# Three of eight output tiles: expert rows gated by diagonal matrices on TensorE, added in one VectorE instruction

## The reference

```python
xf = layernorm(x).reshape(-1, 512)                       # 1024 tokens
probs = softmax(gelu(xf @ wg1 + bg1) @ wg2 + bg2)[:, :20] # 20 experts
top_vals, top_idx = top_k(probs, 2)
gates = zeros((N, 20)).at[arange(N)[:, None], top_idx].set(top_vals)
for e in range(20):
    y = y + gates[:, e, None] * (xf @ We[e] + be[e])
x = x + y
```

## Time and profile before

| | |
|---|---|
| three timed runs | 677.53, 674.92, 677.24 us (median 677.24) |
| the profiled execution | 675.09 us |
| its span, first to last instruction | 673.2 us |
| TensorE busy | 642.6 us, 95% of the span |
| VectorE busy | 439.9 us, 65% |
| ScalarE busy | 327.2 us, 49% |
| GpSimd busy | 299.4 us, 44% |
| mean granted clock of TensorE | 0.985 of full speed |

### The profile page before, as it was taken

The page is one execution under the profiler, slowest core; times in us unless marked ns, Lnnn a source line. Parts: engine busy times, 40 slices in busy tenths (PEclk is TensorE's granted clock), DMA queues, the critical chain, the costliest instruction groups (busy, mean ns, idle before and its releaser), DMA issues.

```text
span 673.2 us, 16124 instructions
## 1 busy us (share of the span) xinstructions
PE 642.6 (95%) x6390; PEld 526.1 (78%) x6390; DVE 439.9 (65%) x999; ACT 327.2 (49%) x620; POOL 299.4 (44%) x265
## 2 busy tenths in 40 slices
PE   5999999999999999999999999999999999999980
PEld 5778888887888788887888788887778787788850
DVE  4865666666556555757555557454477678999976
ACT  4435453544434444444433426334355654899930
POOL 2215644366344644366344614612126157788520
PEclk9999999999999999999999999999999999999995
DMA  8512566545764456445753562220000497999729
GB/s 331 210 50 47 137 168 150 128 113 137 174 137 122 121 147 148 111 125 144 174 127 77 136 168 83 80 64 2 2 18 34 146 363 272 382 389 354 285 86 339
DMA packets 41817, 105.68 MB, mean 157 GB/s; under 512 B 8052, under 2 KB 8436, under 8 KB 40962
## 3 DMA queue, kind: packets, MB, share of 16 engines
q1 hardware_dynamic: 37330, 96.12, 48.5%
q0 software_dynamic: 4400, 8.41, 3.4%
HBM read 65.61 MB, written 11.34 MB: 114 GB/s over the span
## 4 chain that ended last, share of the span: by engine, by line
PE 91%; DVE 4%; DMA 2%; ACT 1%; issue 1%; POOL 0%; POOLq 0%; DVEq 0%; SPq 0%; ACTq 0%
PE bank L195 25%; PE bank L197 23%; PE bank L196 23%; PE bank L415 5%; PE bank L397 4%; PE bank L201 3%; DVE x_sb L1854 2%; PE bank L633 1%; PE bank L620 1%; PE bank L649 1%; DMA wr<-scratch_ys 1%; DMA raw<-in_wk 1%; DMA xi<-scratch_xn,row 1%; PE bank L447 1%; DVE stats L1580 0%
## 5 line engine op out<-in xcount | busy, mean ns | idle before, releaser
L1891 POOL TENSOR_SCALAR pp<-pp,rl 128x400 f32<-128x400 f32 x128 | 164.1, 1300 | 182.4 <-DVE rl L1359 182.4
L978 ACT ACTIVATE pp<-pp,acc 128x400 f32<-128x400 f32 x128 | 79.0, 619 | 66.6 <-DVE acc L1418 66.6
L1418 DVE CUSTOM_DVE_ANT_0 pp<-bank,cap 128x400 f32<-128x400 f32 x128 | 65.9, 571 | 50.9 <-PE bank L397 50.9
L195 PE MATMUL bank<-chi,wk 128*128 128x400 f32 x248 | 87.3, 352 | 0.0
L196 PE MATMUL bank<-clo,wk 128*128 128x400 f32 x248 | 85.5, 345 | 0.0
L197 PE MATMUL bank<-chi,wk 128*128 128x400 f32 x248 | 85.5, 345 | 0.0
L1410 DVE STREAM_TRANSPOSE raw<-pp 128x512 f32<-128x512 f32 x128 | 83.4, 688 | 2.2 <-POOL pp L1891 2.2
L195 PE MATMUL bank<-wv,chi 128*128 128x512 f32 x192 | 78.8, 410 | 0.0
L196 PE MATMUL bank<-wv,chi 128*128 128x512 f32 x192 | 75.4, 393 | 0.0
L197 PE MATMUL bank<-wv,clo 128*128 128x512 f32 x192 | 75.2, 392 | 0.0
L195 PE MATMUL bank<-wh,xu 128*128 128x512 f32 x144 | 59.7, 415 | 0.4 <-ACT hT L912 0.2
(11 more groups left out here) (268 smaller groups left out, 1333.6 us busy)
## 6 DMA issues: line engine op xcount, KB each, us to landing
pt<-raw SPq DMA_DIRECT2D x256, 128.0 KB, 2.4
wr<-in_We SPq DMA_DIRECT2D x13, 1024.0 KB, 12.1
craw<-in_ctx SPq DMA_DIRECT2D x15, 800.0 KB, 4.6
raw<-in_We SPq DMA_DIRECT2D x8, 1024.0 KB, 13.2
acc<-in_We SPq DMA_DIRECT2D x6, 1024.0 KB, 12.6
wr<-scratch_ys SPq DMA_DIRECT2D x8, 512.0 KB, 8.1
x_sb<-in_x SPq DMA_DIRECT2D x2, 1024.0 KB, 11.5
scratch_xn<-acc SPq DMA_DIRECT2D x8, 256.0 KB
```

Of the source, the lines that this page charges most:

```text
L195: pe.matmul(o, lhs[0], rhs[0], start=start, stop=False)
L978: act.activation(frame(p8), frame(p8), ACT.Exp, bias=bias, scale=-1.0, accum_out=total).then_inc(S["a_exp"], 1)
L1418: dve.tensor_tensor_reduce(out=frame(p8), in0=scores[:, p8 % 4, :], in1=cap[:, :], scale=-1.0, scalar=nm[:, b, p8:p8 + 1] if seg else 3e38 ...
L1891: pool.tensor_scalar(frame(p8), frame(p8), rl[:, n % 2, p8:p8 + 1], None, ALU.mult).then_inc(S["g_pn"], 1)
```

## The change

Three tiles of the eight, 2, 4 and 6 (`FULL`), are done in another way. ScalarE makes six 128x128 diagonal matrices after the last expert block: the identity scaled by the gates of row c of tile i. For a tile of `FULL`, TensorE puts the bias product into a bank of its own (3, 4 or 7) and leaves the sum open; when the gather of the tile has landed it adds two float32 products to it, diagonal times `yga[:, i, c]`. VectorE then adds the bank to `x_sb` in one instruction. The other five tiles (`plain`) are done as before. The order of the tiles on VectorE and of the output writes on SyncE becomes 0, 1, 3, 2, 5, 4, 7, 6; the order of the gathers stays 0 to 7. `spare` issues products that nobody reads: two behind each plain bias product, three ahead of each tile of `FULL`.

```diff
+        diag = [cs2[:, 128 * j:128 * j + 128] for j in range(4)] + [mbd[:, j, :] for j in range(2)]
+        FULL, ENDING = (2, 4, 6), (0, 1, 3, 2, 5, 4, 7, 6)
+        plain = [i for i in ENDING if i not in FULL]
...
-                def biases(which):
-                    for i in which:
-                        if i >= 3:
-                            pe.wait_ge(S["v_y"], i - 2)
-                        r = slice(32 * (i % 4), 32 * (i % 4) + E)
-                        pe.matmul(pb[i % 3][:, :], gT[r, i // 4, :], be[r, :], start=True, stop=True).then_inc(S["p_be"], 1)
+                def bias(i, bank, stop):
+                    r = slice(32 * (i % 4), 32 * (i % 4) + E)
+                    return pe.matmul(bank[:, :], gT[r, i // 4, :], be[r, :], start=True, stop=stop)
+
+                def spare(n, bank):
+
+                    for _ in range(n):
+                        pe.matmul(bank[:, :], wh[1][0][:, 0, 0:128], wh[1][0][:, 0, :], start=True, stop=True)
+
+                def ending():
+                    for n, i in enumerate(plain):
+                        if n >= 3:
+                            pe.wait_ge(S["v_y"], n - 2)
+                        bias(i, pb[n % 3], True).then_inc(S["p_be"], 1)
+                        spare(2, pb[7])
+                    pe.wait_ge(S["a_gT"], 1 + 2 * len(FULL))
+                    for n, i in enumerate(FULL):
+                        bias(i, pb[(3, 4, 7)[n]], False)
+                    for n, i in enumerate(FULL):
+                        pe.wait_ge(S["v_y"], len(plain))
+                        spare(3, pb[0])
+                        pe.wait_ge(d_ga[i], 16)
+                        for c in range(2):
+                            last = pe.matmul(pb[(3, 4, 7)[n]][:, :], diag[2 * n + c], yga[:, i, c, :], start=False, stop=(c == 1))
+                        last.then_inc(S["p_be"], 1)
...
                 pe.wait_ge(S["a_gT"], 1)
-                biases(range(8))
+                ending()
...
+            act.wait_ge(S["v_rt"], 8)
+            act.wait_ge(S["v_tok"], 2)
+            for n, i in enumerate(FULL):
+                for c in range(2):
+                    act.activation(diag[2 * n + c], ident, ACT.Copy, scale=gmg[:, c, i:i + 1]).then_inc(S["a_gT"], 1)
...
-            biases(range(8))
-            for i in range(8):
+            biases()
+            for n, i in enumerate(ENDING):
+                if i in FULL:
+                    j = FULL.index(i)
+                    dve.wait_ge(S["p_be"], len(plain) + j + 1)
+                    dve.tensor_tensor(x_sb[:, i, :], x_sb[:, i, :], pb[(3, 4, 7)[j]][:, :], ALU.add).then_inc(S["v_out"], 2)
+                    continue
                 dve.wait_ge(d_ga[i], 16)
...
-            for i in range(8):
-                sp.wait_ge(S["v_out"], 2 * i + 2)
+            for n, i in enumerate(ENDING):
+                sp.wait_ge(S["v_out"], 2 * n + 2)
```

More of the change, by code:

```diff
@@ L1804, in gates, with biases @@
                                   ALU.mult).then_inc(S["v_rt"], 1)
[L1806 to L1809, removed]
+            def biases():
+                for n, i in enumerate(plain):
+                    dve.wait_ge(S["p_be"], n + 1)
+                    dve.tensor_tensor(x_sb[:, i, :], x_sb[:, i, :], pb[n % 3][:, :], ALU.add).then_inc(S["v_y"], 1)
             def turn_tokens(n):
@@ L1852, in vector @@
                     if c:
-                        dve.wait_ge(S["v_out"], 2 * i + 1)
+                        dve.wait_ge(S["v_out"], 2 * n + 1)
                     dve.scalar_tensor_tensor(out=x_sb[:, i, :], in0=yga[:, i, c, :], scalar=gmg[:, c, i:i + 1],
```

## The result

The change made the kernel slower: over 19 executions of each, with the runs of both alternating, the ratio of its time to the time of the kernel before is 1.0055, with a 95% interval of 1.0034 to 1.0075. At 677 us that is 3.7 us, between 2.3 and 5.1. The medians are 682.20 us (677.99 to 685.14) and 678.97 us (673.68 to 682.27); the spread of either is larger than their difference, so only the ratio over alternating runs can tell the two kernels apart, not single runs. The profiled execution took 684.66 us, with a span of 682.9 us.

The account below looks back on a forecast made before the run. VectorE and the queue of gathers and writes were taken to bound the ending at the same pace: 2.3 us saved on VectorE return as about 2.5 us of waiting, so 677.24 + 0.14 = 677.4 us, range 674.6 to 680.2.

Parts of the forecast that it names:

- the bound of 0.5%: Whole kernel time: smallest difference from no change that a measurement can tell, about 0.5% or 3.4 us.
- the level: Starting time of the forecast: median of three runs before the change, 677.24 us, to which the difference was added.
- What bounds the ending: Ending, 655 to 671 us: full DMA queue and VectorE run at the same pace; transfer-bound case -0.4 to +0.8 us.
- The new waits for gathers: VectorE in the new tile order: waits of 1.3, 0.65 and 0.55 us for gathers 3, 5 and 7.
- The price of a diagonal pair: TensorE, two float32 products per tile of FULL: 1.9 us at the full clock, 3.5 at the half.
- TensorE, added: Bias and unread products ahead of the first diagonal product: 9.7 us, done at 658.7, before gather 2 at 660.9.
- my own upper bound: TensorE ahead of the first diagonal product, records end to end: 16 x 0.587 + 13 x 0.397 = 14.6 us.
- The second case, TensorE late at the half clock: Diagonal pairs at half clock from 660.9 on: last write 4.7 us later, 681.9 us; chance 0.13.
- its mark: Sign of the half-clock case: VectorE waits for TensorE ahead of tile 4 or 6.
- The aside that it would be 7 us: Half-clock case: 7 us later at 4.2 us a tile or with the clock already down at 653.5.
- The spread of the runs: Whole kernel before the change: three runs with median 677.24 us and a spread of 2.6 us.

Follow-up runs that it names:

- grouped: Changed kernel with unread products regrouped: six after the third plain bias product, 24 after all bias products, three between diagonal pairs; ratio 1.0010, ending 24.5 us.
- only those ahead of the pairs: Changed kernel without the ten unread products behind the plain bias products, three ahead of each diagonal pair kept; ratio 1.0033, endings 24.4 and 25.2 us.

## Why the prediction was wrong

I forecast no change (677.4 us, range 674.6 to 680.2), with 0.13 on slower. The measured median, 682.20, lies outside, and the ratio of 1.0055 is past the bound of 0.5% that I set, though its interval reaches below it. Of the 4.8 us between 677.4 and 682.20, 1.7 are the level: the median before is 678.97 over 19 runs and was 677.24 over three. The rest is the change, and 677.24 + 3.7 = 680.9 would lie outside too.

*What bounds the ending: right.* That the queue of gathers and writes runs beside VectorE at the same pace, so that 2.2 us less on VectorE bring nothing, is shown from both sides: less VectorE alone gives 24.7 us against 24.2, and with half the gathers the same saving shows in full.

*The new waits for gathers: right,* where TensorE does not interfere: 1.3, 0.65 and 0.55 us forecast, 2.23, 0.54 and 0.49 us measured with the products grouped. Gather 3 came as forecast, 13.25 us behind the start (664.72 - 651.47) for 662.3 - 649.0 = 13.3; the first wait is longer because VectorE began the tiles 8.0 us behind the start and not 9.1. Behind the last gather VectorE took 2.13 us (670.02 to 672.15), forecast 2.15.

*The price of a diagonal pair: right.* 1.9 us at the full clock, 3.5 at the half, both taken between two bounds; measured 1.98 (grouped) and 3.5 (only those ahead of the pairs).

*"TensorE, added": the step that failed.* I priced the products ahead of the first diagonal product at two thirds of 16 x 0.587 + 13 x 0.397, 9.7 us, all at the full clock, and wrote that the fifth plain addition would come at 655.7, 6.7 us behind the start. In the chain it was 18.5 us from the first bias product to the first diagonal product (653.80 to 672.30), and the fifth addition came 12.1 us behind the start. Two things were in it.

First, a factor of two thirds for overlap was taken over all records alike. The trace of before had the overlap only between bias products that follow one another directly, six records in 1.13 us:

```profile
648.98 1.13 PE L769 MATMUL bank<-be,gT 20*128 20x512 f32 x6
```

The experiment without unread products has it again; with unread products between them each takes 1.05 us. So an insertion between two overlapping products cost the overlap here as well as itself. Here the Trainium skill, "TensorE: Matmul & The Clock Gate", section "Part 3: Packing small matmuls — row/col tiling", says that products with few rows run at the same time where they lie in different groups of 32 rows. The runs agree: the bias products that ran together lie at different groups, and those with a 128-row product between them did not run together.

Second, the price at the half clock was asked for in the diagonal pairs and never in this step: from the third bias product on each takes 2.00 us and two unread ones 1.15. At my own upper bound, end to end at the full clock, it would have been 14.6 us; no bound that I gave reached 18.5.

How much is either? By the chain's rows the same order at the full clock would take 5 x (1.05 + 0.67) us for the plain groups, half of 3.71 for the three bias products and 0.69 for three unread ones, an estimate of 11.2 us. So of the 8.8 us that were missing, 1.5 are lost overlap and about 7 the half clock. But neither alone made the loss. With no insertions and a clock that fell 3.2 us behind the start, TensorE was done with its bias products at 5.7 us and the ratio was 0.9996; with the clock at 1.00 and the insertions grouped it was 1.0010. And 11.2 us at the full clock would still be ahead of gather 2, which landed 11.9 us behind the start before. No run has the broken order with the clock at 1.00 throughout, so that last part is worked out and not shown; the second profile of the changed kernel, in which one group more ran at the full clock, has an ending 1.5 us shorter.

*The second case, TensorE late at the half clock: the right direction, mostly another mechanism.* Its time, 681.9 us, is near the measured one, and its mark, a wait of VectorE for TensorE, was there. But it laid the price on three slow pairs behind gather 2. In the changed kernel the first pair took 2.52 us in the chain and the others 1.72 and 1.73. With the unread products gone, one pair and most of a second ran at half, and that cost nothing in time (ratio 0.9996); the last pair took 1.88 us, so the clock was back ahead of tile 6, as I had argued against this case. The delay was made in the bias products at the front and the unread products between them, which were to keep the clock up. That 681.9 is so near 682.20 is luck: it is 677.24 + 4.7, where the level was 1.7 us too low and the change cost 3.7. The aside that it would be 7 us with the clock already down at 653.5 was the nearest to it.

*The spread of the runs: too small.* I carried the level of three runs with a spread of 2.6 us; over 19 runs it was 8.6 us. In the two profiles before the endings differ by 0.3 us and their starts by 2.0, so most of it seems to lie ahead of the ending; two profiles do not show that for all runs.

## What to carry to other kernels

Products that nobody reads were free here in one group where TensorE waits anyhow. Put between small products that run beside one another they took the overlap away; the clock fell all the same, and at the half clock the serial work made TensorE the bound. Before an engine is relieved, look at what else runs at its pace: an engine with no wait in the timeline and a queue with a share of 1.0 beside it are two bounds, and taking from one alone brought nothing here. A wait that an insertion may fill has to be counted at both clocks, from the first instruction that is inserted and not from the one that the change is about.

## What the runs showed of the hardware

- The granted clock fell although every bias product (20 rows) was followed by two products of 128 rows and 512 columns, TensorE having no idle time in its row (2.00 of 2.00 us busy in 655 to 657): 2.9 us behind the first bias product in one profile of the changed kernel and 5.1 in the other. Without the unread products it fell 3.2 us behind it, and in the kernel before 4.2, so the pairs did not clearly hold it. With six and then 24 such products in a row it stayed at 1.00 until TensorE's last product.
- A float32 product with 128 rows and 512 columns: two take 1.98 us at a granted clock of 1.00 (grouped) and 3.5 us at 0.50 (only those ahead of the pairs).
- The last write landed 2.0 us behind its issue in the changed kernel, whose queue had run empty, 3.0 us before, and 3.5 us with the grouped products, whose last write is issued 20.7 us behind the start, as before. In the first profile with the unread products only ahead of the diagonal pairs it was issued 20.1 us behind the start and took 3.9 us.
